# Expert tiles rotated over three buffers instead of two, and row scatters in consecutive gaps

## The reference, cut to what matters

```python
h = _layernorm(x) * (1 + ca) + sa
x = x + ga * attn(h)          # gate, conv, selective scan over 16 states, Wo
h = _layernorm(x) * (1 + cb) + sb
logits = h @ router_w.T; top_w, top_idx = top_k(softmax(logits), 2)
g = einsum('th,eih->tei', h, gate_w); u = einsum('th,eih->tei', h, up_w)
y = einsum('tei,ehi,te->th', silu(g) * u, down_w, w_te)    # inner size 352
x = x + gb * y
```

## Time and profile before

| | us |
|---|---|
| median of 3 runs (lowest, highest) | 689.32 (687.8, 689.67) |
| the profiled execution: its time, and the span of its instructions | 686.06, 684.3 |
| busy in the span: PE, PEld, DVE, ACT, POOL | 618.2, 518.8, 552.9, 532.9, 507.5 |
| mean granted TensorE clock | 0.977 |

### The profile page before, as it was taken

One profiled execution on the slowest core, in us unless ns is written; L12 is line 12 of the kernel. 1 busy time (PEld: TensorE's weight loads), 2 busy tenths in 40 slices (PEclk: granted clock), 3 DMA queues, 4 the chain that ended last, 5 costly groups with the idle time before them and its releaser, 6 DMA issues.

```text
span 684.3 us, 14573 instructions
## 1 busy us (share of the span) xinstructions
PE 618.2 (90%) x4473; PEld 518.8 (76%) x4473; DVE 552.9 (81%) x1165; ACT 532.9 (78%) x996; POOL 507.5 (74%) x487
## 2 busy tenths in 40 slices
PE   8988789989989998998998998769789999999995
PEld 6447667867857766786786777658678899999994
DVE  4568797899899999989899999999975586555554
ACT  3689977979998997998999799797834756665650
POOL 5249889877899898899989989977946557644441
PEclk9999999999999999999999999999999999999998
DMA  7303334545634643344544445475612223222545
GB/s 242 125 2 95 95 95 129 157 110 177 208 108 126 172 127 106 117 126 122 158 106 108 107 131 160 118 192 131 176 34 58 65 65 86 82 65 65 154 148 196
DMA packets 65195, 82.93 MB, mean 121 GB/s; under 512 B 6960, under 2 KB 55152, under 8 KB 61024
## 3 DMA queue, kind: packets, MB, share of 16 engines
q1 hardware_dynamic: 59648, 70.78, 38.1%
q0 software_dynamic: 4320, 9.12, 4.0%
q10 hardware_dynamic: 1152, 2.10, 0.8%
HBM read 52.19 MB, written 29.78 MB: 120 GB/s over the span
## 4 chain that ended last, share of the span: by engine, by line
PE 35%; ACT 28%; DVE 14%; issue 11%; POOL 9%; DMA 1%; DVEq 0%; SPq 0%; ACTq 0%; POOLq 0%
PE psum L606 24%; ACT S L1071 10%; PE psum L610 10%; ACT dA L1079 10%; DVE ring L1466 7%; POOL ring L576 5%; POOL S L555 2%; POOL token_rows L477 1%; ACT xn L982 1%; ACT L1019 1%; ACT soft L1010 1%; DMA ring<-results 1%; ACT h2r L1044 1%; ACT soft L1019 1%; ACT soft L1012 1%
## 5 line engine op out<-in xcount | busy, mean ns | idle before, releaser
L576 POOL TENSOR_TENSOR ring<-ring,Cb 128x1024 f32<-128x1024 f32 x128 | 279.2, 2182 | 46.0 <-DVE ring L1466 45.4
L610 PEld LDWEIGHTS psum<-ident,S 128*128 128x128 f32 x1024 | 120.9, 144 | 111.7 <-issue 54.4
L610 PE MATMUL psum<-ident,S 128*128 128x128 f32 x1024 | 161.3, 282 | 41.9 <-POOL S L555 17.3
L1079 ACT ACTIVATE dA<-delta,A 128x512 f32<-128x512 f32 x256 | 178.3, 715 | 10.5 <-DVE ring L1466 10.3
L1071 ACT ACTIVATE S<-duT,BT 128x256 f32<-128x256 f32 x384 | 166.4, 500 | 22.3 <-issue 13.3
L610 PE MATMUL psum<-ident,ring 128*128 128x128 f32 x1088 | 161.3, 280 | 4.0 <-DMA ring<-results 3.7
L1466 DVE TENSOR_TENSOR_SCAN ring<-dA,state,psum 128x512 f32<-128x512 f32 x128 | 157.8, 1266 | 2.5 <-PE psum L610 1.9
L1466 DVE TENSOR_TENSOR_SCAN ring<-dA,psum 128x512 f32<-128x512 f32 x128 | 150.0, 1205 | 2.5 <-PE psum L610 2.2
L610 PEld LDWEIGHTS psum<-ident,ring 128*128 128x128 f32 x1088 | 131.2, 146 | 5.0 <-DMA ring<-results 4.2
L598 POOL DMA_INDIRECT results<-xn,result_at x71 | 68.8, 969 | 74.6 <-DVE xn L1583 64.9
L606 PE MATMUL psum<-uT,S 128*128 128x128 f32 x852 | 107.1, 275 | 1.0 <-DVE uT L1561 1.0
(11 more groups left out here) (218 smaller groups left out, 726.8 us busy)
## 6 DMA issues: line engine op xcount, KB each, us to landing
Cb<-c_rows SPq DMA_DIRECT2D x32, 1024.0 KB, 6.0
token_rows<-zeros SPq DMA_DIRECT2D x64, 272.0 KB, 7.1
uT<-token_rows SPq DMA_DIRECT2D x71, 68.0 KB
ring<-results SPq DMA_DIRECT2D x8, 512.0 KB, 4.9
xT<-in_xT SPq DMA_DIRECT2D x4, 512.0 KB, 5.0
out_T<-xT ACTq DMA_DIRECT2D x8, 256.0 KB, 2.3
stage<-in_xT SPq DMA_DIRECT2D x6, 256.0 KB, 7.1
gateup_w<-in_gate SPq DMA_DIRECT2D x1, 1408.0 KB, 8.3
```

What stands on the lines that cost most here:

```text
L576: nc.gpsimd.tensor_tensor(ring[:, k % RING, :, 0:BANK], ring[:, k % RING, :, 1:], Cb[:, group_ % 2, own, :].unsqueeze(1).to_broadcast([P, ...
L610: return nc.tensor.matmul(out, block_in, ident[at, at], is_transpose=True, start=start, stop=True, skip_group_check=True)
L1079: nc.scalar.activation(dA[:, (k * HALVES + a) % DA_SLOTS, :], delta[:, s % 2, a, :], ACT.Exp, scale=A[:, a, n:n + 1]).then_inc(da_ready, 1)
```

## The change

Every expert buffer becomes three deep (`DEEP = 3`), and so do the PSUM homes: gate in banks 2, 3 and 6, up in 4, 5 and 1. The transpose loses its own bank and goes into the last quarter of a gate bank, the down product loses its own banks and goes into the last quarter of the up bank of the same tile. Silu and `innerT` move to the area of the decays. Because of the shared bank, `up_product(k)` now waits until the weighting of tile `k-3` has read its down product (`o_read`).

The orders of the engines change. TensorE: gate `k`, up `k`, transpose of `k+2`, down `k-2`. VectorE: silu times up of `k`, `turned(k+2)`, `result_places(k+2)`, the weighting of `k-2`. ScalarE: silu of `k`, then `copy_weights(k+2)`. Ahead of the first gap of the tail TensorE now runs the gate and up products of tiles 0 and 1 and three transposes among the last three `add_state` steps; before, it ran gate 0, the three steps, up 0. VectorE has the three `turned` and the first two multiplies among its gaps 0 to 5. The sixth segment's eight row scatters stand in gaps 9 to 16 of the last window instead of 9, 11, ... 23.

```diff
-XS_SLOTS = 4
+XS_SLOTS, DEEP = 4, 3
...
         def PG(k):
-            return bank(2 + k % 2)
+            return bank((2, 3, 6)[k % DEEP])
+        def PX(k):
+            return PG(k if k else DEEP - 1)[:, NIN * P:BANK]
         def PU(k):
-            return bank((4, 1)[k % 2])
+            return bank((4, 5, 1)[k % DEEP])
         def PO(k):
-            return bank((5, 0)[k % 2])[:, 0:P]
+            return PU(k)[:, NIN * P:BANK]
...
-                    i, rest = divmod(gap - 9, 2 if window == SEGS - 1 else 3)
+                    i, rest = divmod(gap - 9, 1 if window == SEGS - 1 else 3)
@@ TensorE @@
+            def turn_row(k):
+                slot, rnd = k % XS_SLOTS, k // XS_SLOTS
...
+                pe.wait_ge(xs_loaded[slot], 16 * (rnd + 1))
...
+                wait(pe, silu_ready, k - DEEP + 1)
+                turn(PX(k), xs[:, slot, 0:HID]).then_inc(xt_filled, 1)
...
-            def up_product(k, par):
-                wait(pe, inner_ready, k - 1)
+            def up_product(k):
+                wait(pe, o_read, k - DEEP + 1)
...
-            def tile(k, par, rnd):
...
+            def tile(k):
+                if k == 0:
+                    gate_product(2)
+                if k == 1:
+                    turn_row(3)
+                    down(0)
+                if 2 <= k < TILES:
+                    if k > 2:
+                        gate_product(k)
+                    up_product(k)
+                if 2 <= k < TILES - 2:
+                    turn_row(k + 2)
+                if k >= 3:
+                    down(k - 2)
@@ ScalarE @@
+            def tile(k):
+                if k == 1:
+                    copy_weights(3)
+                if 2 <= k < TILES:
+                    activate(k)
+                if 2 <= k < TILES - 2:
+                    copy_weights(k + 2)
@@ VectorE @@
+            def tile(k):
+                if 2 <= k < TILES:
+                    inner(k)
+                if 1 <= k < TILES - 2:
+                    turned(k + 2)
+                    result_places(k + 2)
+                if k == 1:
+                    weighted(0)
+                if k >= 3:
+                    weighted(k - 2)
```

More of the change, by code:

```diff
@@ L323, in tile_schedule @@
             for t in range(TILES + 2):
[L324 removed]
                 if t < TAIL_TILES:
                     beside(2 * t)
[L327 removed]
+                tile(t)
                 if t < TAIL_TILES:
@@ L904, in down @@
                 pe.wait_ge(inner_ready, k + 1)
-                wait(pe, o_read, k - 1)
-                if k == 1:
-                    pe.wait_ge(read["prefix"], EARLY_SEGS + 1)
                 for c, (i0, w) in enumerate(INNER):
-                    last = product(PO(par), innerT[0:w, par % 2, c * P:(c + 1) * P],
+                    last = product(PO(k), innerT[0:w, k % DEEP, c * P:(c + 1) * P],
                                    down_w[0:w, c, ds(e * HID, HID)], c == 0, c == NIN - 1)
@@ L923, in combine @@
                 last.then_inc(mt_filled, 1)
-            def tile(k, par, rnd):
[L927 to L939, removed]
+            def tile(k):
[12 more added lines that the diff above has]
+                    down(k - 2)
             pe.wait_ge(group[0], GROUP_STEPS[0])
-            pe.wait_ge(xs_loaded[0], 16)
-            turn(PX, xs[:, 0, 0:HID]).then_inc(xt_filled, 1)
+            turn_row(0)
             pe.wait_ge(loaded["gateup"], 32)
             pe.wait_ge(scanned, STEPS * HALVES)
[L946 to L950, removed]
+            gate_product(0)
+            turn_row(1)
+            for a in range(HALVES):
+                add_state(STEPS - 3, a)
+            up_product(0)
+            gate_product(1)
+            for a in range(HALVES):
+                add_state(STEPS - 2, a)
+            up_product(1)
+            turn_row(2)
+            for a in range(HALVES):
+                add_state(STEPS - 1, a)
             for gap in range(TAIL_GAP):
@@ L1133, in _, with copy_weights, activate @@
             act.wait_ge(group[0], GROUP_STEPS[0])
-            def copy_weights(k, par):
+            def copy_weights(k):
                 if k == FULL_TILES:
                     act.wait_ge(group[1], GROUP_STEPS[1])
-                wait(act, u_filled, k - 1)
+                wait(act, u_filled, k - DEEP + 1)
                 e = act.value_load(expert[0:1, ds(k, 1)], min_val=0, max_val=EXPERTS - 1)
[L1140 to L1150, removed]
+                nc.scalar.copy(both_w[:, k % DEEP, :], gateup_w[:, ds(e * 2 * INTER, INTER + NIN * P)]).then_inc(weights_copied, 1)
+            def activate(k):
+                act.wait_ge(g_filled, k + 1)
+                wait(act, inner_ready, k - DEEP + 1)
+                nc.scalar.activation(silu[:, k % DEEP, :], PG(k)[:, 0:NIN * P], ACT.Silu).then_inc(silu_ready, 1)
+            def tile(k):
[5 more added lines that the diff above has]
+                    copy_weights(k + 2)
+            copy_weights(0)
+            copy_weights(1)
+            activate(0)
+            copy_weights(2)
+            activate(1)
             def combine(h):
@@ L1555, in beside, with turned @@
                 gap_work(gap % GAPS, SEGS + gap // GAPS)
-            def turned(k, par):
+            def turned(k):
                 dve.wait_ge(xt_filled, k + 1)
-                wait(dve, u_filled, k - 1)
-                V.tensor_copy(xsT[:, par % 2, :], PX).then_inc(xt_read, 1)
+                wait(dve, u_filled, k - DEEP + 1)
+                V.tensor_copy(xsT[:, k % DEEP, :], PX(k)).then_inc(xt_read, 1)
             def result_places(k):
@@ L1571, in result_places, with inner, weighted @@
                                 ).then_inc(places_read, 1)
[L1573 to L1589, removed]
+            def inner(k):
+                dve.wait_ge(silu_ready, k + 1)
+                dve.wait_ge(u_filled, k + 1)
+                wait(dve, o_filled, k - DEEP + 1)
+                V.tensor_tensor(innerT[:, k % DEEP, :], silu[:, k % DEEP, :], PU(k)[:, 0:NIN * P], ALU.mult).then_inc(inner_ready, 1)
+            def weighted(k):
+                slot, rnd = k % XS_SLOTS, k // XS_SLOTS
+                at = k % (2 * XS_SLOTS)
+                dve.wait_ge(o_filled, k + 1)
+                wait(dve, given[slot], 16 * rnd)
+                dve.wait_ge(places_read, 2 * (k + 1))
+                V.tensor_scalar(ob[:, slot, :], PO(k), row_weight[:, at:at + 1], None, ALU.mult).then_inc(o_read, 1)
+            def tile(k):
[8 more added lines that the diff above has]
+                    weighted(k - 2)
             def combine(h):
@@ L1597, in _ @@
             for gap in range(TAIL_GAP):
-                if gap == 3:
-                    turned(0, 0)
+                if gap == 0:
+                    turned(0)
+                if gap == 1:
+                    turned(1)
+                gap_work(gap, SEGS)
+                if gap in (3, 5):
+                    inner((gap - 3) // 2)
+                if gap == 4:
+                    turned(2)
                 if gap == TAIL_GAP - 1:
-                    result_places(0)
-                gap_work(gap, SEGS)
+                    for k in range(DEEP):
+                        result_places(k)
             tile_schedule(dve, tile, beside, combine)
```

28 lines of the change are left out of this document (17 added, 11 removed).

## The result

The changed kernel took **706.64 us** (median of 4, 704.69 to 709.24) against 688.56 (4 runs, 686.75 to 689.67) for the kernel before in the same comparison: ratio 1.0261, interval 1.0223 to 1.0298. The forecast was 700.1, with a range of 690.0 to 704.5. The direction was right; the loss is 18.1 us instead of 10.8, and above the range. The profiled execution took 706.3 us (span 704.4), 20.1 us of span more than that of before.

A forecast was written before the change was run, and what follows sets the result against it. TensorE's weight loads were taken to fill the steady stretch, so a third buffer could only cost there. -1.6 + 2.9 + 8.2 + 1.3 = +10.8 us on 686.06 gave 696.9; 3.26 us to the median, 700.1; range 690.0 to 704.5.

The forecast's parts named there:

- Steady tiles: Tiles 19 to 70: up waits for the weighting through the shared bank, 2.28 us a tile against 2.124, +8.2 us.
- the loop through VectorE's queue: Steady tiles: up(k) holds up(k+1) through VectorE's multiply, turned, places and weighting, 2.28 us a tile.
- the one through the down product: Steady tiles: second loop of up, transpose, down product, weighting and back to up, without VectorE's queue, 2.23 us.
- a VectorE without a queue would not hide the wait: Steady tiles: product latency, weighting and handovers exceed gate k+1's 0.67 us, even without VectorE's queue.
- Head: Start to up(3): earlier scatters and first rows let gate 0 start near 500.5, -1.6 us (-3 to 0).
- No scan is held: Head: step 8's multiply ends at 485.7, TensorE needs it near 486.5, so packed scatters delay no scan.
- POOL's burst holds the scans: Rival, head: step 8's product comes later than 486.5, slip adds up to 2.5 us, 702.6; chance 0.03.
- scans that end after 500: Head: sign that the burst was dear, if the last segment's scans end after 500.
- Tiles 3 to 19: up(3) to up(19), beside the last segment's tail: 44.2 us instead of 41.27, +2.9 us (0 to +5).
- normalised turn: Tiles 3 to 19: the tile with the tail's normalised turn, forecast at 2.57 us.
- ScalarE's order: Tiles 3 to 19: weight copies, 0.81, between silu and modulation; rows' turn 3.14 (TensorE waits 0.6), logits 3.87.
- End: Behind the last up: three down products instead of two, third scatter starts at 5.3 against 4.02 us, +1.3 us.

The follow-up runs named there:

- e6: Changed kernel with TensorE's register read of the down product's expert moved ahead of the tile's gate product: 703.55 us, ratio 1.0211 to the kernel before.
- e3: Changed kernel with VectorE's rows' copy, places and weighting of tile k-2 ahead of silu times up of tile k: 706.04 us, ratio 1.0264.
- e2: Changed kernel with the sixth segment's row scatters back in every other gap: 706.87 us, ratio 1.0271 to the kernel before.
- e8: Changed kernel with the edits of e1, e2 and e7 together: 689.88 us against 689.07 for the kernel before, ratio 1.0021.
- e10: e8 with VectorE's residual sum of the last segment taken one gap earlier: 690.51 us against 688.96 for the kernel before, ratio 1.0025.
- e11: Kernel before with GpSimd's second square root one tile earlier and the residual sum xT one gap earlier: 687.38 us against 688.96, ratio 0.9983.
- e12: e11 with the sixth segment's scatters in each gap and that window's square root two gaps earlier: 686.75 us against 688.41 for the kernel before, ratio 0.9976.
- e1: Changed kernel with the down product in a PSUM bank of its own, so up no longer waits for the weighting: 698.88 us, ratio 1.0154.
- e7: Changed kernel with ScalarE copying weights ahead of the activation again and GpSimd's second tail square root one tile earlier: 702.58 us, ratio 1.0189.
- e5: Kernel before with only the sixth segment's scatters packed, one in each gap: 691.78 us against 689.07, ratio 1.0041.
- e9: e8 with the sixth segment's scatters in each gap again: 691.67 us against 688.96 for the kernel before, ratio 1.0046.
- e4: e3 with the down product's expert register read at the tile's start, ahead of the gate product: 698.96 us, ratio 1.0171 to the kernel before.

## Why the prediction was too low

- **Steady tiles (+8.2, measured +8.77).** The mechanism, a loop through the shared bank, was right; the loop that binds was not the one named. The prediction put the loop through VectorE's queue at 2.28 and the one through the down product at 2.23. It is the other way round: the handover from the weighting to `up` takes 0.05 to 0.06, not 0.12, which makes the first 2.23 (e6); the second lacked the register read, some 0.14 ahead of the down product, which makes it 2.29. The two errors, of 0.06 and 0.14, nearly cancelled, so that the size came out by luck. Its remark that a VectorE without a queue would not hide the wait is what e3 showed.
- **Head (-1.6, measured +1.57).** The failed step is "No scan is held". It followed GpSimd's multiplies alone and left out the square root, which stands in the same queue at gap 19 and for which VectorE waits in order. From the start of the four scans to the end of the last scan pass 15.75 to 15.77 us in all six profiled executions with looser scatters or the earlier root (before, e2, e8, e10, e11, e12), and 17.71 to 18.36 in all eight with packed scatters and the root at gap 19. The rival "POOL's burst holds the scans" had the effect, but at 0.03 and with the product as the link. Its sign, scans that end after 500, came (503.53), but does not tell by itself: in e11, without packed scatters, they end at 501.84. Of the 3.2 us missed, 2.6 are the held scans (1.84 of it the row's wait) and 1.1 lay ahead of any change in that execution; 0.5 were won back. That the gain was larger than forecast goes with the clock: it stayed at 1.00 from 505 to 510, and `up(3)` came 14.10 us after the first gate load. In e1, e6, e7 and e8, with the same order of tiles at a mean clock of 0.70 to 0.81 there, it came 15.7 after.
- **Tiles 3 to 19 (+2.9, measured +5.98).** Tile by tile, from `up` to `up`, forecast and measured: residual 4.0 and 3.95, normalised turn 2.57 and 4.54, rows 3.14 and 3.54, logits 3.87 and 4.28, exp 3.73 and 3.62, routing 2.43 and 2.42, prefix sums 3.22 and 3.40, second table 2.98 and 2.98. The failed step is the normalised turn: 2.57 has no wait in it, though the kernel before already waited 0.50 there and took 3.08 for this tile. It is again GpSimd's square root, here behind the scatters of results, of which each waits for a weighting that now comes later. ScalarE's order was seen but sized 0.8 us too small over rows and logits.
- **End (+1.3, measured +1.38)** was right. The 2.41 us of the reload behind it are no effect of the change as far as the runs show: e5, which has the tiles and the reload of the kernel before, took 16.48 us from the last scatter to the end, e11 and e12 14.40 and 14.72. The second half followed the first by 3.94 us here and in e7, by 3.65 in e5, and by 1.5 to 2.4 in all others; what decides it stays open.
- **The sum.** By ratios: bank 1.07%, order 0.72%, both together 2.15% (e9), scatters 0.25% (e8 against e9), rest 0.21%. The bank and the order give 0.36%, 2.5 us, more together than singly; four intervals of 0.2 to 0.4% each way stand behind this figure. In the profiled executions the excess lies in tiles 3 to 19: the bank gives 0.1 us there alone (e1) and 2.1 on top of the order (e9 against e7), and 1.6 of the difference is e1's one tile at the lower clock. No run tests this. Of the rest, 1.4 us with an interval that begins at zero, nothing is shown.

## What to carry to other kernels

Before packing work into an engine's queue, list everything else that the queue issues in that stretch, small operations above all: here 1.3 us of square root, which ended 2.9 us later against the scans than before, held the scans of another engine. Where a buffer shares its PSUM bank with a later stage's product, and the program lets the next product in only when that stage's last reader is done, a third buffer holds no more than that: here a tile took 2.29 us so, and 2.12 with a bank of its own. The same scatters cost 2.7 us in e5 and nothing once the root stood two gaps earlier (e12). Where the order of an in-order engine changes, price the change at each place where another engine waits for it, not only in the steady loop.

## What the runs showed of the hardware

A register read behind a blocked wait on TensorE's queue cost 0.13 us a tile: e3 and e4 differ in its place alone, and their steady tiles took 2.291 and 2.165 us (between the two loads around it 0.23 to 0.25 against 0.12). From the end of the weighting to the weight load that waited for it passed 0.05 to 0.06 us in the steady tiles; the 0.12 behind `turned` in the earlier trace rows is another pair of instructions. The lower clock came in e1 behind waits of 2.25, 0.95 and 1.19 us (0.66 from 545 to 550) and in e4 behind 2.10, 0.95 and 1.19 (0.83 from 540 to 550). It did not come in the changed kernel behind 1.82, 0.86 and 1.19, nor in e6 behind 2.03, 0.96 and 1.30 (both 1.00 from 540 to 555). So the length of these waits alone does not tell.
